# An attention and mixture-of-experts layer on one core: leaner projections, and the maxima's rows by one transpose and a DMA

## The reference

```python
xn = layernorm(x)
# attention, 16 heads of 16, causal
q, k, v = split(xn @ Wqkv.T)
q, k = q * cos + rotate_half(q) * sin, k * cos + rotate_half(k) * sin
attn = softmax(where(causal, -inf, q @ k.T * D ** -0.5)) @ v @ Wout.T
# feed-forward: 32 experts of width 128, 6 per token, and a shared one of width 256
scores = sigmoid(xn @ gate_w.T)
w, idx = top 6 of the 4 best groups of 4 experts
y = sum over the token's experts of w * (silu(xn @ w11.T) * (xn @ w33.T)) @ w22.T
shared = silu(xn @ sw1.T) * (xn @ sw3.T) @ sw2.T
return x + attn + y + shared
```

## Time and profile before

| | us |
|---|---|
| median of 3 runs | 922.68 (922.35 to 1379.95) |
| profiled execution | 912.92 |
| its span, first to last instruction | 910.9 |
| PE busy | 832.9 (91%) |
| DVE busy | 621.0 (68%) |
| ACT busy | 496.9 (55%) |
| POOL busy | 501.1 (55%) |

### The profile page before, as it was taken

The page is one execution under the profiler, slowest core; times in us unless marked ns, Lnnn a source line. Parts: engine busy times, 40 slices in busy tenths (PEclk is TensorE's granted clock), DMA queues, the critical chain, the costliest instruction groups (busy, mean ns, idle before and its releaser), DMA issues.

```text
span 910.9 us, 17583 instructions
## 1 busy us (share of the span) xinstructions
PE 832.9 (91%) x5282; PEld 454.6 (50%) x5282; DVE 621.0 (68%) x1247; ACT 496.9 (55%) x1214; POOL 501.1 (55%) x636
## 2 busy tenths in 40 slices
PE   2799987698989999989999999988999999999997
PEld 1466654233343433368888887863343343433444
DVE  4778887878876787755555555546788777888322
ACT  2456543154656566634445444445676767667662
POOL 5445640399998503056667666526888888800000
PEclk9999997789999999999999999998999999999999
DMA  7005544610000132047778777874585555600011
GB/s 220 0 31 178 192 155 141 187 53 18 1 19 1 26 80 71 1 127 238 221 223 248 232 228 243 131 115 75 73 174 91 71 88 72 91 7 1 13 37 45
DMA packets 81792, 96.11 MB, mean 106 GB/s; under 512 B 12835, under 2 KB 73251, under 8 KB 81699
## 3 DMA queue, kind: packets, MB, share of 16 engines
q0 software_dynamic: 19968, 31.47, 19.4%
q1 hardware_dynamic: 44838, 46.75, 17.3%
q10 hardware_dynamic: 16896, 16.78, 5.4%
HBM read 61.11 MB, written 33.82 MB: 104 GB/s over the span
## 4 chain that ended last, share of the span: by engine, by line
PE 52%; issue 16%; DVE 11%; DMA 7%; POOLq 6%; POOL 4%; ACT 2%; DVEq 1%; ACTq 0%
PE bank L1183 12%; PE bank L1166 12%; PE vector_banks L1142 10%; DMA turned<-normed_rows,tok_i 6%; DVE mpart L948 6%; POOLq L567 5%; PE vector_banks L1055 4%; PE vector_banks L1034 3%; PE bank L1055 3%; POOL turned L575 2%; PE vector_banks L1203 2%; POOL slot_w L569 2%; PE bank L1071 2%; PE bank L1169 1%; PE vector_banks L1145 1%
## 5 line engine op out<-in xcount | busy, mean ns | idle before, releaser
L948 DVE TENSOR_REDUCE mpart<-vector_banks 128x2 f32<-128x1024 f32 (+3 forms) x320 | 330.6, 1062 | 94.4 <-PE vector_banks L1142 54.3
L698 ACT ACTIVATE probs<-bank 128x512 f32<-128x512 f32 (+3 forms) x428 | 213.6, 537 | 132.0 <-PE bank L1166 63.7
L1166 PE MATMUL bank<-turned 99*128 99x512 bf16 (+3 forms) x640 | 207.8, 357 | 13.6 <-ACT probs L698 4.5
L575 POOL DMA_INDIRECT turned<-normed_rows,tok_i x128 | 125.3, 979 | 131.1 <-PE vector_banks L1034 81.5
L1142 PE MATMUL vector_banks<-turned 96*128 96x512 bf16 (+3 forms) x640 | 185.7, 360 | 11.3 <-DVE mpart L948 10.8
L590 POOL DMA_INDIRECT res<-expert_rows,slot_i x96 | 148.8, 1550 | 39.8 <-issue 28.4
L1166 PEld LDWEIGHTS bank<-turned 99*128 99x128 bf16 x640 | 59.0, 98 | 182.0 <-ACT probs L698 87.1
L698 ACT ACTIVATE at_first<-bank 128x512 f32<-128x512 f32 (+3 forms) x212 | 106.3, 531 | 71.9 <-PE bank L1169 36.8
L1261 PE MATMUL vector_banks<-xn_all,probs 128*128 x512 | 135.0, 386 | 4.5 <-issue 1.7
L1183 PE MATMUL bank<-probs,V 128*32 128x512 f32 (+3 forms) x856 | 101.9, 548 | 0.0
L1261 PEld LDWEIGHTS vector_banks<-xn_all,probs 128*128 128x128 f32 x512 | 87.2, 190 | 17.3 <-issue 9.3
(11 more groups left out here) (153 smaller groups left out, 997.1 us busy)
## 6 DMA issues: line engine op xcount, KB each, us to landing
expert_rows<-probs ACTq DMA_DIRECT2D x32, 512.0 KB, 4.4
term_rows<-at_first SPq DMA_DIRECT2D x96, 128.0 KB
turned<-term_rows SPq DMA_DIRECT2D x32, 384.0 KB, 4.7
xn_all<-wexp SPq DMA_DIRECT2D x32, 384.0 KB, 4.0
normed_rows<-xn_all SPq DMA_DIRECT2D x4, 512.0 KB, 5.5
turned<-normed_rows,tok_i POOLq DMA_INDIRECT x128, 3.8
out<-res SPq DMA_DIRECT2D x16, 128.0 KB, 1.7
res<-x SPq DMA_DIRECT2D x1, 1536.0 KB, 8.7
```

The costliest lines, as they stand in the source:

```text
L575: gp.indirect_dma_start(xg[:, n % XR, :], None, xn_dram, bass.IndirectOffsetOnAxis(ap=tok_i[:, n:n + 1], axis=0)).then_inc(rows_in[n % XR] ...
L698: A(PT[v // 2 % 6][:, v % 2, 0:width], bank[A_BANK[step][0]][:, 0:width], ACT.Exp).then_inc(s["scalar_bank_read"], 1)
L948: V.tensor_reduce(mpart[:, t % TPC, 2 * j:2 * j + 2, p], ring[:, :, 0:w], AX.X, ALU.max).then_inc(s["vector_bank_read"], 1)
L1166: last = mm(ring[:, 0:CH - off], k_turned(parity(g), slice(0, KM), h, kb * P, P), q_turned(slice(0, KM), h, c * CH + off, CH - off), start ...
```

## The change

- The memset of the ones leaves POOL; SP copies them from `onesb` by a DMA.
- The rotation takes three products that cover q and k at once, not six.
- ACT's copy of the gate is scaled by 0.5; `hm` stays on DVE, `hb` becomes a product on POOL (`gated_up`), behind the tile's `split_terms` (for the last tile ahead of it).
- One mask in bf16 serves for both.
- `mt` is one transpose of 48 columns; DVE copies 48x128 to `turned_max` (two buffers), and SP's `store_max` writes that to the three rows of the query array by a DMA, on which the chunk's first `st` now waits. The query array is laid out chunk by chunk, so those rows are contiguous.
- `mt` stands two steps behind `mc`; in group 0 a chunk's strips must be done six steps ahead of its first score step, not four; and a waiting `pv` goes ahead of a chunk's first score step.
- `store_max` calls are placed in SP's queue.

```diff
@@ -102,8 +102,7 @@
...
-        score_goals.append((4 * (key_blocks.index((0, c, 0)) - 1), len(scores)))
-    score_goals[-1] = (4 * (key_blocks.index((0, NCH - 1, 0)) - 1), len(scores))
+        score_goals.append((4 * key_blocks.index((0, c, 0)) - 6, len(scores)))
@@ -136,7 +135,7 @@
...
-                    later.append((at + 4, ("mt", *step[1:3])))
+                    later.append((at + 2, ("mt", *step[1:3])))
@@ -161,6 +160,8 @@
...
+        if kb == 0 and len(pending) == 2:
+            values(pending.pop(0))
         order.append(("st", g, c, kb, 0))
@@ -345,7 +345,8 @@
...
-            return QK[rows, j * T + q0:j * T + q0 + w]
+            at = q0 // CH * HG * CH + j * CH + q0 % CH
+            return QK[rows, at:at + w]
@@ -365,7 +366,8 @@
...
-        mcat = sb("mcat", [P, TPC * HG, 3], BF16)
+        mcat = sb("mcat", [P, KM - KQ, TPC * HG], BF16)
+        turned_max = [sb(f"turned_max{b}", [(KM - KQ) * TPC * HG, P], BF16) for b in range(2)]
@@ -414,17 +416,33 @@
...
+            sp.wait_ge(s["ident_made"], 1)
+            sp.dma_start(QK[KQ:KM, HG * T:2 * HG * T].rearrange("p (a n) -> p a n", n=P),
+                         onesb[0:KM - KQ, :].unsqueeze(1).to_broadcast([KM - KQ, HG * T // P, P])).then_inc(s["ones_made"], 16)
...
-                at, arrived = (0, q_in[c]) if kind == 0 else ((1 + parity(g)) * HG * T, k_in[parity(g)][c])
...
+                if kind == 0:
+                    to = QK[0:KQ, c * HG * CH:(c + 1) * HG * CH].rearrange("p (h q) -> p h q", q=CH)
+                else:
+                    to = QK[0:KQ, (1 + parity(g)) * HG * T:(2 + parity(g)) * HG * T].rearrange("p (h q) -> p h q", q=T)
+                    to = to[:, :, c * CH:(c + 1) * CH]
+                arrived = k_in[parity(g)][c] if kind else q_in[c]
+                sp.dma_start(to, term_rows[kind, g * HG:(g + 1) * HG, :, :, c * CH:(c + 1) * CH].rearrange("h s d t -> (s d) h t")
...
+            def store_max(g, c):
+
+                sp.wait_ge(s["vector_bank_read"], D_AT["mt", g, c] + 1)
+                m = MC_AT["mc", g, c]
+                if m:
+                    sp.wait_ge(s["max_stored"], 16 * m)
+                sp.dma_start(QK[KQ:KM, c * HG * CH:(c + 1) * HG * CH], turned_max[m % 2][:, :]).then_inc(s["max_stored"], 16)
@@ -436,6 +454,8 @@
                 sp.dma_start(rows[:, :, 0:D], xn_all[:, quarter * QT4:(quarter + 1) * QT4, :]).then_inc(s["xn_stored"], 16)
                 if quarter:
                     store_weights(quarter - 1)
+                if quarter == 3:
+                    store_max(0, 0)
@@ -471,23 +491,32 @@
...
             for c in range(NCH):
+                if c + 1 < NCH:
+                    store_max(0, c + 1)
+                if c == NCH - 1:
+                    store_max(1, 0)
                 used(0, c)
                 load_terms(0, 1, c)
             for c in range(NCH):
                 load_terms(1, 2, c)
             for c in range(NCH - 1):
+                store_max(1, c + 1)
                 used(1, c)
                 load_terms(0, 2, c)
             with sp.Fori(1, E // NB) as i:
                 for b in range(NB):
                     load(NB * i + b, b)
+            store_max(2, 0)
             used(1, NCH - 1)
             load_terms(0, 2, NCH - 1)
             for c in range(NCH):
                 load_terms(1, 3, c)
             for c in range(NCH):
+                store_max(*((2, c + 1) if c + 1 < NCH else (3, 0)))
                 used(2, c)
                 load_terms(0, 3, c)
+            for c in range(1, NCH):
+                store_max(3, c)
...
-            gp.drain()
-            gp.memset(QK[KQ:KM, HG * T:2 * HG * T], 1.0).then_inc(s["ones_made"], 1)
...
+            def split_terms(t, b):
...
+            def gated_up(t, b):
+                gp.wait_ge(s["hm_ready"], t + 1)
+                if t >= 2:
+                    gp.wait_ge(s["hT_psum"], t - 1)
+                gp.tensor_tensor(hb[b][:, :], hm[b][:, :], u1[b][:, :], ALU.mult).then_inc(s["act_ready"], 1)
+                gp.drain()
+
+            for t in range(NT - 1):
+                split_terms(t, t % 2)
+                gated_up(t, t % 2)
+            gated_up(NT - 1, (NT - 1) % 2)
+            split_terms(NT - 1, (NT - 1) % 2)
...
-                copy(g1[b][:, :], bank[3 + b][:, D:2 * D])
+                A(g1[b][:, :], bank[3 + b][:, D:2 * D], ACT.Copy, scale=0.5)
...
-                for c in range(2):
-                    yc = y[:, c * D:(c + 1) * D].rearrange("p (h d) -> p h d", d=DH)
-                    V.tensor_tensor(rope_c[:, c * D:(c + 1) * D].rearrange("p (h d) -> p h d", d=DH), yc,
...
-                    for odd in range(2):
-                        last = V.tensor_tensor(
-                            rope_s[:, c * D:(c + 1) * D].rearrange("p (h d) -> p h d", d=DH)[:, :, odd::2],
-                            yc[:, :, 1 - odd::2],
-                            sn[:, c, odd::2].unsqueeze(1).to_broadcast([P, H, DH // 2]), ALU.mult)
...
+                V.tensor_tensor(heads(rope_c[:, :]), heads(y), ct.unsqueeze(2).to_broadcast([P, 2, H, DH]), ALU.mult)
+                for odd in range(2):
+                    last = V.tensor_tensor(heads(rope_s[:, :])[:, :, :, odd::2], heads(y)[:, :, :, 1 - odd::2],
+                                           sn[:, :, odd::2].unsqueeze(2).to_broadcast([P, 2, H, DH // 2]), ALU.mult)
...
-                    dve.wait_ge(s["hT_psum"], t - 1)
+                    dve.wait_ge(s["act_ready"], t - 1)
...
-                                       op0=ALU.add, op1=ALU.mult)
-                dve.drain()
-                V.scalar_tensor_tensor(out=hb[b][:, :], in0=hm[b][:, :], scalar=0.5, in1=u1[b][:, :],
-                                       op0=ALU.mult, op1=ALU.mult).then_inc(s["act_ready"], 1)
+                                       op0=ALU.add, op1=ALU.mult).then_inc(s["hm_ready"], 1)
+                dve.drain()
@@ -847,10 +881,9 @@
...
-                V.tensor_scalar(pick[:, tiles, :], ex[:, tiles, 0:E], PICKED, None, ALU.is_equal)
...
-                V.tensor_tensor(wgt[:, tiles, :], pick[:, tiles, :], sig[:, tiles, :], ALU.mult)
...
+                V.tensor_tensor(wgt[:, tiles, :], pickb[:, tiles, :], sig[:, tiles, :], ALU.mult)
...
-                        V.tensor_reduce(mneg[:, :].rearrange("p (t h) -> p t h", h=HG), mpart[:, :, :, 0:c + 1], AX.X, ALU.max)
+                        V.tensor_reduce(mneg[:, :].rearrange("p (h t) -> p t h", h=HG), mpart[:, :, :, 0:c + 1], AX.X, ALU.max)
                         dve.drain()
-                        V.tensor_scalar(mcat[:, :, 0], mneg[:, :], -1.0, None, ALU.mult)
+                        V.tensor_scalar(mcat[:, 0, :], mneg[:, :], -1.0, None, ALU.mult)
...
-                        V.tensor_copy(QK[KQ:KM, 0:HG * T].rearrange("p (h q) -> p h q", q=T)[:, :, c * CH:(c + 1) * CH],
-                                      ring[KQ:KM, :, :].rearrange("p a b -> p (a b)").bitcast(BF16).rearrange("p (h q) -> p h q", q=CH)
+                        m = MC_AT["mc", g, c]
+                        if m >= 2:
+                            dve.wait_ge(s["max_stored"], 16 * (m - 1))
+                        V.tensor_copy(turned_max[m % 2][:, :], ring[0:(KM - KQ) * TPC * HG, 0, 0:P // 2].bitcast(BF16)
...
-                        for j in range(HG):
-                            for t in range(TPC):
-                                k = j % 2 * TPC + t
-                                last = turn(ring[KQ:KM, j // 2, :].bitcast(BF16)[:, k * P:(k + 1) * P],
-                                            mcat[:, t * HG + j, :], identb[:, :])
-                        last.then_inc(full, 1)
+                        turn(ring[0:(KM - KQ) * TPC * HG, 0, 0:P // 2].bitcast(BF16), mcat[:, :, :].rearrange("p a b -> p (a b)"),
+                             identb[:, :]).then_inc(full, 1)
...
-                            pe.wait_ge(s["vector_bank_read"], D_AT["mt", g, c] + 1)
+                            pe.wait_ge(s["max_stored"], 16 * (MC_AT["mc", g, c] + 1))
```

More of the change, by code:

```diff
@@ L312, in layer @@
         top = routing([P, NT, 8])
-        pick = routing([P, NT, E])
         pickb = routing([P, NT, E], BF16)
@@ L383, in layer @@
         names = """x_in w_in tables_in w2_in xn_stored ident_made counts_made
-            var_ready root_ready scales_ready xn_ready qk_ready xT_psum xT_ready proj_done rope_done proj_read act_ready hT_psum hT_ready
+            var_ready root_ready scales_ready xn_ready qk_ready xT_psum xT_ready proj_done rope_done proj_read act_ready hm_ready hT_psum hT_ready
             shared_done shared_added terms_made terms_turned terms_read terms_stored ones_made ones_in
@@ L388, in layer @@
             vector_bank_full vector_bank_read scalar_bank_full scalar_bank_read
-            v4_ready mcat_ready pv_done o_read
+            v4_ready max_stored mcat_ready pv_done o_read
             exp_x_psum exp_x_ready gu_done gate_ready exp_h_ready exp_hT_psum exp_hT_ready y_done y_read weights_in written""".split()
@@ L463, in _ @@
```

(30 more changed lines are left out.)

3 lines of the change are left out of this document (removed).

## The result

| | before | after |
|---|---|---|
| median, us | 922.51 | 950.57 |
| range of the runs, us | 919.43 to 1379.95 | 945.54 to 951.97 |
| profiled execution, us | 912.92 | 950.59 |
| its span, us | 910.9 | 948.6 |
| PE busy / idle in the span, us | 832.9 / 78.0 | 851.6 / 97.0 |

The ratio is 1.0308, with a 95% interval of 1.0284 to 1.0332. The forecast was 916.7 us in 905 to 927, so the result lies outside on the slow side. The profiled execution of before was 10 us under its median. The gap of the two spans is therefore 37.7 us, while that of the medians is 28.1. The one run of before at 1379.95 us was a slow execution and is left out of the ratio.

The account below looks back on a forecast made before the run. PE was taken as the limit nearly everywhere, with DVE and mutual waits setting the pace from 147 to 180 us. Terms -6.2 - 1.5 + 0.3 + 6.0 - 6.9 + 2.3 = -6.0 gave 916.7 us, range 905 to 927.

Parts of the forecast that it names:

- start, L803: At the start, ScalarE's op L803 no longer slowed beside POOL's memset, so PE's first product comes earlier: -6.2 us.
- late statistics, end of projections: Outside the projection loop, DVE's lighter rotation and gate bring late statistics and the last addition sooner: -1.5 us.
- projection loop, POOL's slack: In the projection loop, POOL's gate product fits before PE's transposes with 0.4 us of slack per tile: 0.
- transposes' time, 14 chunks: In attention, PE gets back 0.99 us per chunk from fewer transposes; 14 chunks, bound -13.9 us.
- waits for the maxima, 14 x 0.5: In attention, transposes two steps behind the maxima make PE wait 0.5 to 1.1 us; 0.5 net gain taken per chunk.
- (0,1), SP's queue: At chunk (0,1), the maxima's DMA stands behind plan_ready and four weight loads, delaying the first score: +6.0 us.
- DMA at (0,2), (0,3), (2,1), (2,3), (3,3): At these chunks, first scores wait for the small DMA, at (2,1) behind five loads: +2.3 us together.
- rival D: At (0,1), plan_ready 3.7 us later, PE's clock low 5 us longer, landing later: +5.7, 922.4 us; chance 0.13.
- part 3: In attention, the maxima's rows by one transpose, a small copy and a DMA per chunk: +1.7 us.
- rival C: At the start, L803 is slow for a reason other than the memset: 922.9 us; chance 0.08.
- rival A: In the projection loop, POOL's gate product comes late and PE pays in 14 tiles: +11, 927.7 us; chance 0.09.
- B: In attention, PE never waits for the maxima and (0,1)'s rows are early: -18.3, 904.4 us; chance 0.15.

Follow-up runs that it names:

- e1: Kernel before with only the ones copied by a DMA in place of POOL's memset: 917.14 us, ratio 0.9947.
- e2: Kernel before with the ones by DMA, three rotation products, gate product on POOL and one mask; maxima's transposes and order as before: 914.07 us, ratio 0.9920.
- e12: Kernel before with fifteen of sixteen transposes left out per chunk, DVE's copy reading the one sixteen times (maxima's rows not the reference's): 913.26 us, ratio 0.9895.
- e5: Changed kernel (two steps) with store_max(0,1) on SP ahead of the plan's wait and the weight loads: 942.60 us, ratio 1.0234.
- e6: Changed kernel with four steps instead of two, and store_max(0,1) ahead of the plan's wait and the weight loads: 913.98 us, ratio 0.9922.
- e3: Changed kernel with the maxima's transpose four score steps behind them instead of two: 921.59 us, ratio 1.0001.
- e8: Changed kernel with four steps, store_max(0,1) first, group 0's strips due eight steps ahead, last group's key loads behind store_max(2,1): 904.47 us, ratio 0.9820.
- e10: The kernel of e8 with six steps instead of four between maxima and transpose: 906.66 us, ratio 0.9810.

## Why the prediction was wrong, by its own steps

| step | forecast, us | measured, us |
|---|---|---|
| start, L803 | -6.2 | -4.9 (e1) |
| late statistics, end of projections | -1.5 | -3.1 (e1 to e2, not resolved) |
| projection loop, POOL's slack | 0 | +0.5 (ten tiles: 65.38 for 64.88) |
| transposes' time, 14 chunks | -13.9 | -9.2 for 16 (e12) |
| waits for the maxima, 14 x 0.5 | +7 | +28.6 (e5 to e6) |
| (0,1), SP's queue | +6.0 | +6.8 to +8.0 (e5, e6) |
| (0,0) | +0.3 | +0.5 (2.88 for 2.42 us) |
| DMA at (0,2), (0,3), (2,1), (2,3), (3,3) | +2.3 | 2.6 of wait, all at (2,1) |

With the transposes at 14/16 of 9.2, the measured column comes to about +24 us, against +28.1; 4 us are not traced to a step.

**The step that failed** is the passage "Two steps are worth 1.4 us of PE's time ..., 2 or more where a value block falls between. ... I take 0.5 net per chunk". It counts the wait for the maxima at +7 us; it measured +28.6. DVE's side of it was right, 2.5 us. PE's side was wrong in two ways.

First, the 0.7 us a step was an average over whole key blocks, in which strips and value products are counted. The gap in question begins where a chunk's strips end, so it holds the score products of two steps and little else: at (3,3), where the steps are short, PE has done them 0.40 us after the last strip (881.14 to 881.54). PE waited 1.3 to 2.5 us at most chunks. The mean of the waits for L999 is 1.7 (23.7 in 14), above the upper bound of 1.1 that the text had set. That bound came from the average step, too.

Second, the clock. The forecast used it at (0,1) (rival D) and for no other stop, although showed half the clock behind such a stretch from 182 to 188. Between e5 and e6 it is 15.0 of 27.4 us. The Trainium skill (TensorE: Matmul & The Clock Gate, HAM oscillation) tells of a kernel whose waits between groups of matmuls let each next group start at the low clock, so that a wait costs more than its length. Those waits are longer than the stops here; the rows of this case show the same fall behind shorter ones, with PE wholly busy at 0.50 after a stop of 2.33 us, though not behind each (behind the 1.82 us at 672.44 it stays at 1.00). The earlier trace rows alone was reason enough to make two steps a rival on the slow side with a real chance. The chance given to slower, 0.03, was too small: the text had an upper bound on the waits, and none on what follows them.

Third, and smaller: PE's time was counted at its length because PE was busy 97% of late attention. At the place where the time was taken away, PE was waiting for a bank that DVE reads. By the medians of e12 six tenths of it came off (9.2 of 15.8 us, with the interval a third to nine tenths), by the traces of late attention a quarter (0.26 us a chunk of 0.99). With four steps and the early store, part 3 gains nothing: e6 and e2 differ by 0.1 us.

**What was right.** L803 took 0.17 us and PE's first projection began at 11.60 (forecast 11.4), so rival C falls; the overlap with the memset was the cause. The loop kept its 13.0 us for two tiles but for half a microsecond in ten, and PE's one wait for POOL, at tile 0, stands ahead of it: rival A falls. POOL's product took 0.73 us for the forecast's 0.6, and 0.97 at tile 0, beside a DVE op. B falls with the 23.7 us of waits. At (0,1) the mechanism was right, a wait released by the DMA and SP's queue, and the edit that removes it was worth 6.8 to 8.0 us, inside the bounds of 3 to 9.

**What was luck.** The forecast put the first score of (0,1) at 190.9, and it came at 190.81. But 190.9 was counted on the time axis of before, without the 7.7 us that the forecast itself took off ahead of it. Counted from the transposes of (0,0), the score comes 47.2 us later for 36.3 before, 10.9 more, where the forecast had 8.4. The weight loads start 34.9 us behind those transposes for 28.8: 6.1 later, where the forecast took 2.5 and at most 3.7. With the clock at 0.53 from 187 to 198 this is rival D's course.

Part 3 as a whole had +1.7 us in the forecast; it measures +36.5 with two steps, +7.5 with four (e3 over e2) and -9.6 in e8.

## What to carry to other kernels

When the distance between a producer and a waiting instruction is shortened, count the instructions that really stand between the two, at that place, and set them against the producer's whole chain; an average step of the loop says nothing there. Stops of 1.3 to 2.5 us on PE that recur cost more here than the idle time they left, 27.4 us for 12.4, through the clock; look at the granted clock right behind each stop before it is priced. An engine that is busy 97% of a stretch can still be waiting at the very place where its work is taken away. A small DMA inherits what its queue carries: with the queue free it took 2.4 us to the product that reads it, behind the bulk loads 11.0.

## What was not expected of the hardware

- **The same code does not lose the same clock.** Up to the first chunk's transposes the changed kernel and e2, e3, e5 to e10 do the same work in the same order. In their profiles (0,0) starts at 138.52 (e8) to 143.59 us (the changed kernel). In e2, which gets there at 139.13, PE's transposes behind the late statistics start at 36.97, against 37.99 in the changed kernel. Both have PE idle for 3.17 us ahead of that. Yet in the changed kernel the granted clock is 0.57 from 36 to 44 us, and the four products at 38.44 take 3.62 us; in e2 it is 1.00 from 33 to 44, and they take 1.88, as in the kernel before. So a position in one profile carries an error of some microseconds, and that is why most terms are taken from medians above.
- **A halt of several engines that the profile doesn't explain.** During the first eight gathers on POOL, ACT and DVE start their next ops late though the products were done, here in the changed kernel:

```profile
363.51 0.49 ACT L736 ACTIVATE probs<-bank 128x384 f32<-128x384 f32 x1 [2.41 <-remote]
...
364.05 0.28 PE L1197 MATMUL bank<-turned 99*128 99x256 bf16 x1 [1.56 <-ACT probs L736]
...
365.65 1.23 DVE L981 TENSOR_REDUCE mpart<-vector_banks 128x2 f32<-128x1024 f32 x1 [3.13 <-PE vector_banks L1177]
```

  From the transposes of (1,2) to those of (1,3) it takes 46.3 us in the profile of before and 51.0 to 58.3 in all thirteen others, e1 and e12 among them, whose order is that of before. So the profile of before happened to miss the halt, which at the 5.4 us that e1 has more is about half of the 9.8 us by which it lay under its median. What the engines wait for stays open; it is no part of the change, and no run was made for it.
